# Decoder layer on one core: four chunks of a feed-forward product moved across an all-engine barrier

## The chip, the cores and the metric

One Trainium2 chip, one of its cores. The metric is the device time of one execution in microseconds (us). TensorE (PE) does matmuls and transposes, ScalarE (ACT), VectorE (DVE) and GpSimd (POOL) the elementwise work, SyncE (SP) issues most DMAs. "PEld" rows are weight loads of TensorE.

## The reference, cut to what matters

Input x is 2 batches of 512 rows of 1024. The layer is:

```python
x = layernorm(x + attention(x))
x = layernorm(x + matmul(fake_quant(x), fake_quant(ctx)))        # called x2 below
h = relu(x @ up_w) ** 2                                          # 1024 -> 2048
routed = (x @ fc1_w) @ expert_w * sum(top2(x @ gate_w)) @ fc2_w  # 1024 -> 512 -> 512 -> 1024
x = layernorm(x + layernorm(h @ down_w + routed, gamma, beta))
```

All of it is float32. The change lies in the first tiles of `x @ up_w`, for batch 0.

## The kernel before, in words

The program has two parts, each a block in which every engine runs a list of its own, and engines wait for one another through semaphores. The first part is attention and cross product (to x2), the second the feed-forward layer. At the end of the first block all engines drain and meet (the profile puts this at line 71), and a second meeting follows that clears semaphores (line 2157). Together they are called the barrier here.

Each factor of a product is split into a rounded part (`_hi`) and the rest (`_lo`), and a product is three matmuls, hi x hi, hi x lo and lo x hi, for every chunk k of 128 of the 1024 contracted columns. A 128 x 512 tile of the hidden layer thus takes 8 chunks x 3 = 24 matmuls into one PSUM bank. Weight tiles are numbered m; tile m sits in slot m % 2 of `u_hi` and `u_lo`. Batches are b.

The first block computes x2 for all 8 row tiles. While its last tiles are still in work, TensorE fills in: it transposes batch 0's rows (`x2T_hi`, `x2T_lo`), computes the routing logits of batch 0 (`first_logits`, 16 matmuls) and the products (m, b) = (0, 0) and (1, 0), each in two halves of four chunks (`first_product(m, part)`). The last of a product's matmuls raises `op_used`.

The second block begins with `first_products`: TensorE transposes batch 1's rows chunk by chunk (`transpose_x1(k)`, four transposes each, into three PSUM banks in turn), ScalarE rounds the chunk (`x1T_hi_out`, line 1645), VectorE subtracts (`x1T_lo_out`, line 1809, raises `x1T_lo_done`), and TensorE contracts it for (0, 1) and (1, 1). A contraction (line 1552) of chunk k waits for `x1T_lo_done` k + 1; a transpose of chunk k >= 3 waits for k - 2, since its bank must have been read. After that the products of tiles 2, 3, ... follow, for both batches, then seven block products (line 1611) in phases p1 to p7.

ScalarE's list at the start of the second block, in the order of the code:

```python
x1T_hi_out(0); x1T_hi_out(1); logits_out(0); x1T_hi_out(2); relu(0, 0)
x1T_hi_out(3); square(0, 0); x1T_hi_out(4); relu(1, 0); x1T_hi_out(5)
square(1, 0); x1T_hi_out(6); x1T_hi_out(7)
```

`relu(m, b)` waits for the `op_used` of its product. `split_u(m)` (ScalarE, then VectorE at line 1813) prepares weight tile m once the slot's former products are over. SyncE loads weight tiles 2 and 3 first thing behind the barrier, and SyncE and GpSimd wait there until the stores of x2 have landed.

Of the kernel before, what the change touches and what calls it, by code (L numbers as in the profile page):

```python
# [33 lines left out]
KT = EMB // P  # L34
# [16 lines left out]
def split_products(stationary, moving):  # L51

    (s_hi, s_lo), (m_hi, m_lo) = stationary, moving
    return ((s_hi, m_hi), (s_hi, m_lo), (s_lo, m_hi))


def attention_and_cross(nc, so, args, x2_dram, w2_dram):
# [13 lines left out]
    with ExitStack() as ctx:  # L71
# [82 lines left out]
        S = {**so["sem"], **{n: sem(n) for n in names}}  # L154
# [162 lines left out]
        def _(pe):  # L317
# [76 lines left out]
            def cross(t):  # L394
                pe.wait_ge(S["q1T_done"], t + 1)
                b = t // BT
                for k in range(CK):
                    for n in range(NH):
                        mm = pe.matmul(xa_ps[:, n * BANK:(n + 1) * BANK], q1T[:, t % 2, k], q2[:, b, k, n * BANK:(n + 1) * BANK],
                                       start=(k == 0), stop=(k == CK - 1))  # L400
                mm.then_inc(S["xa_ready"], 1)
# [34 lines left out]
            def first_logits():  # L436
                pe.wait_ge(S["x2T_lo_done"], KT)
                pe.wait_ge(S["gate_lo_done"], 1)
                gate = so["gate_st"]
                rows = lambda n: tr_ps[0:n, 0:BT].rearrange("p t c -> p (t c)")  # L440
                for k in range(KT):
                    pe.matmul(rows(2 * EXPERTS), gate[:, k], x2T_hi[:, k], start=(k == 0), stop=False)
                    mm = pe.matmul(rows(EXPERTS), gate[:, k, 0:EXPERTS], x2T_lo[:, k], start=False, stop=(k == KT - 1))
                mm.then_inc(S["lgT_ready"], 1)

            def first_product(m, part):
                if part == 0:
                    pe.wait_ge(S["u_lo_done"], m + 1)
                    pe.wait_ge(S["o_done"], TILES)
                acc = sc_ps[:, m * NG * TQ // 2:(m + 1) * NG * TQ // 2].rearrange("p n d -> p (n d)")  # L450
                for k in range(part * KT // 2, (part + 1) * KT // 2):
                    pe.wait_ge(S["x2T_lo_done"], k + 1)
                    st = [so[u][:, m, k] for u in ("u_hi", "u_lo")]
                    for i, (s, v) in enumerate(split_products(st, (x2T_hi[:, k], x2T_lo[:, k]))):
                        mm = pe.matmul(acc, s, v, start=(k == 0 and i == 0), stop=(k == KT - 1 and i == 2))
                if part == 1:
                    mm.then_inc(S["op_used"], 1)
# [81 lines left out]
            transpose_x2(7)  # L539
            cross(7)  # L540
            first_product(0, 1)
            first_product(1, 0)
            first_logits()
            first_product(1, 1)

        @block.scalar
        def _(act):
# [721 lines left out]
def product_index(m, b):  # L1269

    return 2 * b + m if m < 2 else 2 * m + b
# [11 lines left out]
def feed_forward(nc, so, args, x2_dram, w2_dram, t_dram, r_dram, x2b_dram, out):  # L1283
# [8 lines left out]
    with ExitStack() as ctx:  # L1292
# [64 lines left out]
        S = {**so["sem"], **{n: sem("f_" + n) for n in names}}  # L1357
# [155 lines left out]
        def _(pe):  # L1513
            def transpose_x1(k):

                if k >= 3:
                    pe.wait_ge(S["x1T_lo_done"], k - 2)
                for t in range(BT):
                    mm = pe.transpose(x1T_bank(k)[:, t * P:(t + 1) * P], x2_tok[:, t, k * P:(k + 1) * P], ident[:])  # L1519
                mm.then_inc(S["x1T_ready"], 1)  # L1520
# [27 lines left out]
            def contraction(m, b, k):  # L1548

                st = [u[:, m % 2, k] for u in (u_hi, u_lo)]  # L1550
                for i, (s, v) in enumerate(split_products(st, (xT_hi[b][:, k], xT_lo[b][:, k]))):
                    mm = pe.matmul(acc_b[:, product_index(m, b) % 4], s, v, start=(k == 0 and i == 0), stop=(k == KT - 1 and i == 2))  # L1552
                return mm

            def first_products():

                for k in range(3):
                    transpose_x1(k)
                pe.wait_ge(S["u_lo_done"], 2)
                for k in range(KT):  # L1560
                    pe.wait_ge(S["x1T_lo_done"], k + 1)
                    mm = contraction(0, 1, k)
                    if k < 3:
                        contraction(1, 1, k)
                    if k + 3 < KT:
                        transpose_x1(k + 3)
                mm.then_inc(S["op_used"], 1)
                for k in range(3, KT):
                    mm = contraction(1, 1, k)
                mm.then_inc(S["op_used"], 1)  # L1570
# [13 lines left out]
            def tile_step(phase, k, t):  # L1584
# [29 lines left out]
                elif t == BT - 1 and k % 2:  # L1614
                    mm.then_inc(S["d_used"], 1)

            first_products()
            transpose_logits(0)
            for m in range(2, MU):
# [565 lines left out]
```

## Time and profile before

| | |
|---|---|
| median of 3 runs | 629.79 us (627.51, 629.79, 632.41) |
| profiled execution | 629.14 us |
| its span, first to last instruction | 627.3 us |
| TensorE busy | 593.6 us, 95% |
| mean granted TensorE clock | 0.992 |
| barrier, TensorE's last matmul to its first transpose | 206.46 to 207.73 us |

Times in the rows are us from the span's start, durations us unless marked ns. An idle time stands in brackets with what ended it. Ends of matmuls are modelled, their starts are recorded. The span is the part of an execution that the rows cover.

### The profile page before, as it was taken

The page shows a single profiled execution, that of the slowest core. Times are in us where ns is not written, and L with a number is a line of the kernel's source. Part 1 is how long each engine was busy: PE and PEld are TensorE (multiplying, and loading weights), DVE is VectorE, ACT ScalarE, POOL GpSimd, SP SyncE. Part 2 cuts the span into 40 slices and gives each one's busy share as a digit, 9 for nine tenths or more (in the row PEclk, how much of TensorE's full clock was granted, in tenths as well). Part 3 has the DMA queues.
Part 4 walks back from the last instruction along what each step waited for, and adds up shares of the span by engine and source line. Part 5 has one row for each costly group of instructions (what it writes and reads, how often), then busy time and mean ns, then how long its engine had stood idle before and what let it go on. Part 6 is the DMA issues. An engine that isn't in the chain of part 4 may idle for free.

```text
span 627.3 us, 9388 instructions
## 1 busy us (share of the span) xinstructions
PE 593.6 (95%) x3728; PEld 476.8 (76%) x3728; DVE 382.1 (61%) x515; ACT 299.1 (48%) x384; POOL 123.9 (20%) x162
## 2 busy tenths in 40 slices
PE   2799999998999899999999999999999999999993
PEld 1687877666776688788888888888888888888882
DVE  4947898889854355335333331338864565749976
ACT  4556688896684544333333342114344333323824
POOL 2811355735442022422210000000000000021000
PEclk9999999998999999999999999999999999999998
DMA  9766675673663668779998774203433336089913
GB/s 335 286 186 187 183 203 167 170 259 106 194 203 135 241 239 317 263 274 344 315 344 314 252 253 121 77 1 101 135 91 86 94 99 235 1 275 328 293 55 124
DMA packets 82252, 123.61 MB, mean 197 GB/s; under 512 B 23840, under 2 KB 50720, under 8 KB 82208
## 3 DMA queue, kind: packets, MB, share of 16 engines
q1 hardware_dynamic: 74592, 94.95, 45.6%
q0 software_dynamic: 5168, 19.40, 9.3%
q10 hardware_dynamic: 2448, 8.65, 4.3%
q8 instruction: 30, 0.49, 0.3%
q14 instruction: 14, 0.11, 0.1%
HBM read 83.13 MB, written 35.65 MB: 189 GB/s over the span
## 4 chain that ended last, share of the span: by engine, by line
PE 65%; DVE 1%; ACT 0%; issue 0%; ACTq 0%
PE psum L1552 33%; PE psum L1611 30%; PE psum L1519 0%; PE psum L1528 0%; PE psum L1527 0%; PE psum L1545 0%; DVE ffn_lo L1959 0%; DVE ffn_lo L1948 0%; ACT hx L1714 0%; ACT ffn_lo L1724 0%; DVE stat_n L1940 0%; DVE ffn_lo L1933 0%; DVE x1T_lo L1809 0%; PE psum L1536 0%; ACT x1T_hi L1645 0%
## 5 line engine op out<-in xcount | busy, mean ns | idle before, releaser
L1813 DVE TENSOR_TENSOR u_lo<-u_raw,u_hi 128x1024 fp32r<-128x1024 f32 x18 | 24.7, 1373 | 73.7 <-ACT u_hi L1650 73.7
L1552 PE MATMUL psum<-x1T_hi,u_hi 128*128 128x512 f32 x160 | 62.9, 393 | 0.7 <-DVE x1T_lo L1809 0.7
L1552 PE MATMUL psum<-x1T_hi,u_lo 128*128 128x512 f32 x160 | 62.3, 389 | 0.0
L1552 PE MATMUL psum<-x1T_lo,u_hi 128*128 128x512 f32 x160 | 62.3, 389 | 0.0
L1611 PE MATMUL psum<-x2T_lo,x2T_hi 128*128 128x512 f32 x264 | 62.1, 389 | 0.0
L1611 PEld LDWEIGHTS psum<-x2T_lo,x2T_hi 128*128 128x128 f32 x264 | 49.6, 188 | 10.3
L1552 PE MATMUL psum<-x2T_hi,u_hi 128*128 128x512 f32 x144 | 56.5, 392 | 0.0
L1552 PE MATMUL psum<-x2T_lo,u_hi 128*128 128x512 f32 x144 | 56.1, 389 | 0.0
L1552 PE MATMUL psum<-x2T_hi,u_lo 128*128 128x512 f32 x144 | 56.0, 389 | 0.0
L2090 POOL DMA_DIRECT2D x1T_hi<-r_scratch x4 | 2.9, 713 | 243.9 <-PE psum L1611 243.9
L1611 PE MATMUL psum<-x1T_hi,x2T_hi 128*128 128x512 f32 x216 | 50.4, 389 | 0.0
L1611 PE MATMUL psum<-x1T_hi,x2T_lo 128*128 128x512 f32 x216 | 50.4, 389 | 0.0
L341 PE MATMUL psum<-w_hi,xT_hi 128*128 128x512 f32 (+1 forms) x128 | 35.5, 359 | 13.0 <-POOL w_lo L1132 8.2
L1611 PEld LDWEIGHTS psum<-x1T_hi,x2T_lo 128*128 128x128 f32 x216 | 40.5, 188 | 8.4
L1611 PEld LDWEIGHTS psum<-x1T_hi,x2T_hi 128*128 128x128 f32 x216 | 40.5, 188 | 8.4
L1552 PEld LDWEIGHTS psum<-x1T_hi,u_hi 128*128 128x128 f32 x160 | 30.1, 188 | 7.4 <-issue 0.9
L1552 PEld LDWEIGHTS psum<-x1T_hi,u_lo 128*128 128x128 f32 x160 | 30.0, 188 | 6.3
L1552 PEld LDWEIGHTS psum<-x1T_lo,u_hi 128*128 128x128 f32 x160 | 30.0, 188 | 5.9
L341 PEld LDWEIGHTS psum<-w_hi,xT_hi 128*128 128x128 f32 x128 | 20.4, 195 | 18.4 <-issue 8.8
L341 PE MATMUL psum<-w_hi,xT_lo 128*128 128x512 f32 (+1 forms) x128 | 34.3, 349 | 0.0
L341 PE MATMUL psum<-w_lo,xT_hi 128*128 128x512 f32 (+1 forms) x128 | 33.8, 346 | 0.0
L1690 ACT ACTIVATE x2T_hi<-f1b 128x1024 fp32r<-128x1024 f32 x12 | 12.7, 1057 | 39.7 <-PE psum L1611 24.5
(258 smaller groups left out, 1237.3 us busy)
## 6 DMA issues: line engine op xcount, KB each, us to landing
d_raw<-in_L_ffn_down_w_dram SPq DMA_DIRECT2D x20, 512.0 KB, 7.7
t_scratch<-d_raw SPq DMA_DIRECT2D x20, 512.0 KB, 5.1
d_raw<-t_scratch SPq DMA_DIRECT2D x20, 512.0 KB, 3.8
c_sb<-in_ctx_dram ACTq DMA_DIRECT2D x16, 512.0 KB, 3.9
u_raw<-in_L_ffn_up_w_dram SPq DMA_DIRECT2D x16, 512.0 KB, 5.2
r_scratch<-f1b SPq DMA_DIRECT2D x10, 512.0 KB, 4.4
r_scratch<-f2b SPq DMA_DIRECT2D x10, 512.0 KB, 3.1
x_sb<-in_x_dram SPq DMA_DIRECT2D x8, 512.0 KB, 5.8
```

Of the source, the lines that this page charges most:

```text
L341: mm = pe.matmul(qkv_ps[:, c0:c1], s, v, start=(k == 0 and i == 0), stop=(k == KT - 1 and i == 2))
L1552: mm = pe.matmul(acc_b[:, product_index(m, b) % 4], s, v, start=(k == 0 and i == 0), stop=(k == KT - 1 and i == 2))
L1611: mm = pe.matmul(acc_of(phase)[:, t], a, v, start=(k == 0 and i == 0), stop=(k == NP - 1 and i == 2))
L1690: act.activation(oa[oa_slot(s)][:, :, 0], a_raw(phase, j), ACT.Copy).then_inc(S["oa_hi_done"], 1)
L1813: dve.tensor_tensor(u_lo[:, m % 2], u_raw[:, m % 2], u_hi[:, m % 2].bitcast(F32), ALU.subtract).then_inc(S["u_lo_done"], 1)
L2090: pool.dma_start(ob[ob_slot(s)].rearrange("p s h c -> p s (h c)"), r_dram[k * P:(k + 2) * P, n].rearrange("(s p) h c -> p s (h c)", p=P)). ...
```

## The change

`first_product(1, 1)`, chunks 4 to 7 of product (1, 0), leaves the first block, and `first_logits` stands ahead of `first_product(1, 0)`. In the second block the same four chunks are contracted behind the transposes of chunks 0 to 2 of batch 1, and chunk 3 is transposed ahead of the last of them; so the transposes in the loop run four chunks ahead of the contraction and not three.

```diff
@@ -539,9 +539,8 @@
             transpose_x2(7)
             cross(7)
             first_product(0, 1)
+            first_logits()
             first_product(1, 0)
-            first_logits()
-            first_product(1, 1)
@@ -1557,13 +1556,18 @@
                 for k in range(3):
                     transpose_x1(k)
                 pe.wait_ge(S["u_lo_done"], 2)
+                for k in range(KT // 2, KT):
+                    mm = contraction(1, 0, k)
+                    if k == KT - 2:
+                        transpose_x1(3)
+                mm.then_inc(S["op_used"], 1)
                 for k in range(KT):
                     pe.wait_ge(S["x1T_lo_done"], k + 1)
                     mm = contraction(0, 1, k)
                     if k < 3:
                         contraction(1, 1, k)
-                    if k + 3 < KT:
-                        transpose_x1(k + 3)
+                    if k + 4 < KT:
+                        transpose_x1(k + 4)
                 mm.then_inc(S["op_used"], 1)
                 for k in range(3, KT):
                     mm = contraction(1, 1, k)
```

## Rows read from the trace of the kernel before

**Rows 1.** The page: the chain that ended last, shares of the span by line.

```profile
PE psum L1552 33%; PE psum L1611 30%; PE psum L1519 0%; PE psum L1528 0%; PE psum L1527 0%; PE psum L1545 0%; DVE ffn_lo L1959 0%; DVE ffn_lo L1948 0%; ACT hx L1714 0%; ACT ffn_lo L1724 0%; DVE stat_n L1940 0%; DVE ffn_lo L1933 0%; DVE x1T_lo L1809 0%; PE psum L1536 0%; ACT x1T_hi L1645 0%
```

**Rows 2.** Stretches of the span: busy time of each engine, TensorE clock, DMA share, GB/s.

```profile
206.47:207.73 1.26, 0.00 (x1) 0.04 (x1) 0.00 (x0) 0.00 (x0) 0.00 (x0) 1.00 0.00 0
207.73:209.94 2.21, 1.50 (x12) 1.28 (x13) 1.06 (x4) 1.46 (x4) 0.80 (x1) 1.00 0.27 78
209.94:223.98 14.04, 14.01 (x73) 11.12 (x73) 5.83 (x8) 9.35 (x17) 0.81 (x2) 1.00 0.89 325
223.98:616.70 392.72, 392.67 (x1742) 323.23 (x1740) 216.45 (x280) 144.04 (x188) 35.36 (x33) 1.00 0.57 194
```

**Rows 3.** TensorE in order of time: start us, us, line, operation, count, idle before it.

```profile
203.58 0.39 PE L455 MATMUL psum<-x2T_hi,u_hi 128*128 128x512 f32 x1
...
206.07 0.39 PE L455 MATMUL psum<-x2T_hi,u_lo 128*128 128x512 f32 x1
207.73 1.50 PE L1519 MATMUL psum<-ident,f2b 128*128 128x128 f32 x12 [1.26 <-PEq L2157]
209.94 0.47 PE L1552 MATMUL psum<-x1T_hi,u_hi 128*128 128x512 f32 x1 [0.72 <-DVE x1T_lo L1809]
210.25 0.40 PE L1552 MATMUL psum<-x1T_lo,u_hi 128*128 128x512 f32 x1
...
211.18 0.40 PE L1552 MATMUL psum<-x1T_hi,u_lo 128*128 128x512 f32 x1
211.41 0.60 PE L1519 MATMUL psum<-ident,f2b 128*128 128x128 f32 x4
211.77 0.47 PE L1552 MATMUL psum<-x1T_hi,u_hi 128*128 128x512 f32 x1
...
217.33 0.60 PE L1519 MATMUL psum<-ident,f2b 128*128 128x128 f32 x4
...
218.92 0.40 PE L1552 MATMUL psum<-x1T_hi,u_lo 128*128 128x512 f32 x1
219.34 0.50 PE L1552 MATMUL psum<-x1T_hi,u_hi 128*128 128x512 f32 x1
219.68 0.40 PE L1552 MATMUL psum<-x1T_lo,u_hi 128*128 128x512 f32 x1
```

**Rows 4.** Drains at line 71: duration min/median/max in ns, then the start in us.

```profile
L71 ACTq DRAIN  x1: 1271/1271/1271, 197.5 to 197.5; - x1
L71 POOLq DRAIN  x1: 667/667/667, 199.0 to 199.0; - x1
L71 DVEq DRAIN  x1: 853/853/853, 199.7 to 199.7; - x1
L71 SPq DRAIN  x1: 124/124/124, 200.9 to 200.9; - x1
L71 PEldq DRAIN  x1: 4295/4295/4295, 202.2 to 202.2; - x1
```

**Rows 5.** Two stretches around the end of the last store of x2.

```profile
202.00:203.00 1.00, 1.00 (x6) 0.43 (x5) 0.00 (x0) 0.00 (x0) 0.00 (x0) 1.00 0.57 234
203.00:204.00 1.00, 1.00 (x6) 0.65 (x4) 0.00 (x0) 0.00 (x0) 0.00 (x0) 1.00 0.00 0
```

**Rows 6.** VectorE in order of time, ahead of the barrier and behind it.

```profile
192.52 1.22 DVE L931 TENSOR_TENSOR u_lo<-u_raw,u_hi 128x1024 fp32r<-128x1024 f32 x1
...
209.11 2.11 DVE L1809 TENSOR_TENSOR x1T_lo<-psum,x1T_hi 128x512 fp32r<-128x512 f32 x3 [1.05 <-ACT x1T_hi L1645]
...
218.59 0.69 DVE L1809 TENSOR_TENSOR x1T_lo<-psum,x1T_hi 128x512 fp32r<-128x512 f32 x1 [0.43 <-ACT x1T_hi L1645]
221.92 1.23 DVE L1813 TENSOR_TENSOR u_lo<-u_raw,u_hi 128x1024 fp32r<-128x1024 f32 x1 [2.63 <-ACT u_hi L1650]
```

**Rows 7.** TensorE in order of time around 145 us.

```profile
145.43 0.62 PE L381 MATMUL psum<-ident_bf,q 128*128 128x128 bf16 x8 [1.79 <-ACT q L578]
```

**Rows 8.** The stretch behind that: TensorE's busy time, then its granted clock.

```profile
146.00:150.00 4.00, 3.62 (x66) 0.57 0.38 139
```

## Prediction

> **What bounds the kernel now.** I read the chain that ended last first. It is TensorE nearly throughout: the first products (line 1552) and the matmuls of the seven block products (line 1611) make 63% of the span [rows 1]. The windows say how full TensorE is there: from 223.98 to 616.70 it is busy 392.67 of 392.72 us, at a granted clock of 1.00 [rows 2]. So time saved ahead of 223.98 reaches the end whole, and nothing behind that point has slack that could swallow it. The windows ahead of it show what is still to be had: 1.26 us in which TensorE stands at the barrier, then 2.21 us of which 1.50 is busy, then 14.04 us that look full [rows 2]. I then read TensorE in order of time. The barrier's gap lies between the last matmul of `first_product(1, 1)`, which starts at 206.07, and the first transpose at 207.73; twelve transposes follow, and the first contraction starts at 209.94, released by VectorE's `x1T_lo` [rows 3]. A second stall hides in the window that looks full: the matmul before it starts at 218.92, the next at 219.34, where the step is 0.23 [rows 3]. Last, the drains at line 71 say who opens the barrier: ScalarE's ends at 198.8, GpSimd's at 199.7, VectorE's at 200.6, SyncE's at 201.0, TensorE's at 202.2 + 4.3 = 206.5 [rows 4]. TensorE alone holds the barrier for the last 5.5 us.
>
> **Removed ahead of the barrier.** `first_product(1, 1)` is four chunks of three matmuls, 12 in all. From 203.58 to 206.07 are 11 steps, 0.226 each [rows 3]; 12 x 0.226 = 2.72 us. The 16 logit matmuls are moved ahead of `first_product(1, 0)`, on the same engine and at the same cost, with nothing that they read late: VectorE had finished the last of its work for them and for the second weight slot at 192.52 + 1.22 = 193.74 [rows 6], and they would start near 203.58 - 16 x 0.23 - 2.72 = 197.2. With 12 matmuls fewer TensorE arrives at 203.8 and is still 2.8 us behind SyncE, so the barrier opens 2.72 us earlier.
>
> **Added behind it.** The same 12 matmuls, between the transposes of chunks 0 to 2 and the first contraction of batch 1. Their moving rows and weights are ready since before the barrier, so they wait for nothing. There the step is a little longer: 210.25 to 211.18 is four steps, 0.2325 each [rows 3]. 12 x 0.2325 = 2.79 us, 0.07 more than was removed. Each group of four transposes costs 0.36 us to the next matmul (211.41 to 211.77) and 0.08 more at that matmul (209.94 to 210.25 is 0.31 against 0.23) [rows 3]. There are six such groups in both kernels (chunks 0 to 2 together, then 3, 4, 5, 6 and 7), so they cancel.
>
> **The first stall goes.** TensorE waits for chunk 0's transpose, ScalarE's rounding and VectorE's subtraction. How long, a row bounds from two sides. By the modelled end of the transposes it is the 0.72 of the row. By starts it is more: a group of four has 0.60 busy, but its successor starts after 0.36, 0.24 before that end; so the twelve, 1.50 busy, would let a matmul start at 207.73 + 1.50 - 0.24 = 208.99, and the stall is 209.94 - 208.99 = 0.95 us [rows 3]. I take 0.95, since starts are observed and a successor was seen to start ahead of the modelled end. [...]
>
> **The second stall goes too, if the copies keep pace.** Chunk 7's transposes start at 217.33 and its contraction at 219.34, 2.01 us later, with 9 matmuls between them (218.59 + 0.69 = 219.28 is the end of VectorE's last `x1T_lo`) [rows 3, 6]. The stall is 219.34 - 218.92 - 0.23 = 0.19, and 0.11 more at the matmul behind it (219.68 - 219.34 against 0.23): 0.30 us. After the change the transposes run one chunk further ahead. Counted from the first transpose behind the barrier: transposes of 0 to 2 until 1.26 (0.95 earlier than 2.21); 9 moved matmuls 0.08 + 2.09, to 3.43; chunk 3's transposes to 3.79; 3 moved matmuls to 4.57; six matmuls for k = 0 to 5.97, then chunk 4's transposes; 1.84 each for k = 1 and 2 with their transposes, so chunk 5 at 7.81 and chunk 6 at 9.65; three matmuls, and chunk 7's transposes at 10.79 to 11.15; nine matmuls for k = 4, 5, 6, to 13.32. Chunk 7 is ready at 10.79 + 2.01 = 12.80: 0.52 us of slack where there was none. The other waits in that stretch have more: chunk 3's transposes need `x1T_lo` of chunk 0, ready at 2.21 (before: 209.94), at 3.43; k = 6 starts at 12.62 and needs 9.65 + 2.01 = 11.66.
>
> **Waits and queues that move.** One wait becomes real: ScalarE's `relu(1, 0)` waits for the second `op_used`, which was up before the barrier and now comes at about 4.8 on the scale above. ScalarE reaches it behind its copy of chunk 4, whose transposes start at 5.97, so near 7.2: no wait, and the square and the copies of 5 to 7 queued behind it are not held. TensorE's product of the third weight tile needs `u_lo`, written at 221.92 + 1.23 = 223.15 against a start of 223.98, 0.83 to spare [rows 2, 6]; it hangs on the end of contraction (0, 1), behind which the same 15 matmuls and 4 logit transposes follow as before, so the 0.83 stays. Every load that SyncE or GpSimd issues behind the barrier starts 2.72 us earlier while its reader moves by less, so none gets later. They wait for the stores of x2; DMA is busy 0.57 of the stretch from 202 to 203 and nothing from 203 to 204 [rows 5], and the barrier would open at 207.73 - 2.72 = 205.0. I cost all of this at nothing; if that cover were gone, up to the 0.52 and 0.83 would be eaten before anything shows.
>
> **The sum.** 0.95 + 0.30 - 0.07 = 1.18 us. The profiled execution took 629.14 (span 627.3 and 1.8 around it); it would take 627.96. The median of the three runs is 629.79, 0.65 above the profiled one, so I forecast 628.6. Bounds of the gain: 0.65 (0.72 - 0.07, the second stall unchanged) to 1.25 (no loss in the step), so 628.5 to 629.1.
>
> **Rivals.**
> [...]
> Another engine opens the barrier. Then the 12 matmuls are added and not moved: 2.72 - 1.18 = 1.54 us slower, 631.3. That is the price if some drain ends at 206.5; from 205.0 (203.8 + 1.18) on the change loses. The latest is at 201.0 [rows 4], so this is unlikely.
> The copies fall behind: ScalarE does the same list in a shorter time after the transposes come. If chunk 7 is 0.5 us late beyond its slack, about the size of the stall now, the gain is near 0.7: 629.1.
> Nothing is gained, since a wait that I did not see (`u_lo` of the third tile, a weight load) ends last again at 223.98: 629.8. For it speaks only that the stall's place would move; against it the 0.83 and the earlier loads.
>
> **How the numbers follow.** Forecast 0.60 (628.6); copies behind 0.12 (629.1); clock, faster 0.11 (626.9); clock, slower 0.07 (630.3); nothing gained 0.06 (629.8); barrier held 0.04 (631.3). The three runs shown lie from 627.51 to 632.41, so a median can sit a us or two from its place. The range takes in all cases but the last with that scatter: 626.3 to 631.3. About 1% (6.3 us) is what a measurement of this kernel can tell from no change; no case above reaches it, so within 1% gets 0.95, and faster and slower keep 0.02 and 0.03 for what I did not see.
>
> **What would show it.** Right: line 71's TensorE drain ends near 203.8 and is still last; the first transpose starts near 205.0; the first matmul behind the twelve transposes is of the moved product and starts within 1.3 us of it; the first contraction of batch 1 shows no wait for `x1T_lo`, and neither does k = 7; the third tile's product starts near 222.8. Wrong: a drain of another engine later than TensorE's, a clock under 1.00 between 203 and 215, or a start of the third tile's product at 223.9 or later. A difference of several us in the time, with these rows as forecast, would be scatter between runs and not this change.

## The result, and the profile after

| | before | changed |
|---|---|---|
| median | 630.57 us (14 runs, 627.51 to 635.05) | 627.71 us (14 runs, 625.77 to 630.69) |
| profiled execution, its span | 629.14, 627.3 us | 630.69, 628.9 us |

The ratio of changed to before is 0.9964, with an interval from 0.9946 to 0.9981: 1.2 to 3.4 us faster at 630.57. Two further measurements of the same kernel gave 0.9984 (0.9962 to 1.0006) and 0.9974 (0.9954 to 0.9993), so 1.0 and 1.6 us; the first of these two intervals includes 1, which is no change. The gain is small, and the forecast was 1.18. That it is real rests on the stretch D below more than on the medians.

The profiled execution of the changed kernel is, at 628.9, longer than that of the kernel before at 627.3. Whoever compares spans alone sees a loss. The chain that ended last is TensorE as before, with the lines shifted (1552 is now 1551, 1611 is 1615). Shares of the span by line:

```profile
PE psum L1551 33%; PE psum L1615 30%; PE psum L1518 1%; PE psum L1526 0%; PE psum L1527 0%; PE psum L1544 0%; DVE ffn_lo L1963 0%; DVE ffn_lo L1952 0%; ACT hx L1718 0%; ACT ffn_lo L1728 0%; DVE stat_n L1944 0%; DVE ffn_lo L1937 0%; PE psum L1535 0%; ACT root_f L1721 0%; DVE rstd_f L1970 0%
```

Against [rows 1], `DVE x1T_lo` and `ACT x1T_hi`, the copies that TensorE waited for, are gone from the list, and the chain no longer passes through them. The windows that answer to [rows 2], cut at the same events (same columns):

```profile
206.66:207.89 1.23, 0.00 (x0) 0.03 (x1) 0.00 (x0) 0.00 (x0) 0.00 (x0) 1.00 0.00 0
207.89:209.15 1.26, 1.26 (x12) 1.26 (x13) 0.22 (x2) 0.50 (x2) 0.52 (x1) 1.00 0.12 21
209.15:225.63 16.48, 16.48 (x87) 13.45 (x85) 6.67 (x9) 10.29 (x19) 2.47 (x3) 1.00 0.80 286
225.63:618.30 392.67, 392.66 (x1742) 323.23 (x1740) 214.46 (x279) 143.96 (x188) 34.50 (x33) 1.00 0.57 194
```

The barrier's gap is as before (1.23 against 1.26), the transposes behind it are followed at once, and the long window is busy for all of its 16.48 us. Behind 225.63 TensorE is as full as it was, 392.66 of 392.67 us. TensorE in order of time, as in [rows 3]:

```profile
206.27 0.39 PE L455 MATMUL psum<-x2T_hi,u_lo 128*128 128x512 f32 x1
207.89 1.50 PE L1518 MATMUL psum<-ident,f2b 128*128 128x128 f32 x12 [1.24 <-PEq L2161]
209.15 0.47 PE L1551 MATMUL psum<-x2T_hi,u_hi 128*128 128x512 f32 x1
209.47 0.39 PE L1551 MATMUL psum<-x2T_lo,u_hi 128*128 128x512 f32 x1
...
211.31 0.60 PE L1518 MATMUL psum<-ident,f2b 128*128 128x128 f32 x4
211.67 0.48 PE L1551 MATMUL psum<-x2T_hi,u_hi 128*128 128x512 f32 x1
...
212.45 0.40 PE L1551 MATMUL psum<-x1T_hi,u_hi 128*128 128x512 f32 x1
...
218.61 0.60 PE L1518 MATMUL psum<-ident,f2b 128*128 128x128 f32 x4
...
220.89 0.39 PE L1551 MATMUL psum<-x1T_hi,u_lo 128*128 128x512 f32 x1
221.11 0.39 PE L1551 MATMUL psum<-x1T_hi,u_hi 128*128 128x512 f32 x1
...
225.63 0.50 PE L1551 MATMUL psum<-x2T_hi,u_hi 128*128 128x512 f32 x1
```

A moved matmul starts 1.26 us behind the first transpose (207.89 to 209.15) where TensorE stood until 2.21 before. The first contraction of batch 1 (212.45) and the last chunk's (221.11, 0.22 behind the matmul ahead of it) carry no wait. From the first transpose to the third weight tile's product are 225.63 - 207.89 = 17.74 us; before it was 16.25, without the 12 matmuls. The drains at line 71, as in [rows 4]:

```profile
L71 ACTq DRAIN  x1: 1271/1271/1271, 200.4 to 200.4; - x1
...
L71 PEldq DRAIN  x1: 4270/4270/4270, 202.4 to 202.4; - x1
L71 DVEq DRAIN  x1: 853/853/853, 202.6 to 202.6; - x1
L71 SPq DRAIN  x1: 123/123/123, 203.8 to 203.8; - x1
```

TensorE's ends at 206.7, still the last, but now only 2.8 us behind SyncE's at 203.9; it was 5.5. All of them are 3 us later than I had written, since this execution lost time far ahead of the change. At least part of that is TensorE's clock, which fell to 0.50 twice in its first 40 us (in each row: TensorE's busy time, then the mean granted clock, the DMA's share, GB/s):

```profile
22.00:24.00 2.00, 1.54 (x5) 0.59 1.03 395
24.00:26.00 2.00, 2.00 (x12) 0.55 0.45 114
32.00:34.00 2.00, 1.38 (x4) 0.65 0.34 56
34.00:36.00 2.00, 2.00 (x9) 0.50 0.32 50
```

An estimate from these rows is that up to 3.4 us of work are lost (2 x 0.41 + 2 x 0.45 + 2 x 0.35 + 2 x 0.50), where by the same count the execution before lost 1.7, at 146 to 150 [rows 8]. The other 1.2 us or so of the 2.9 us delay are not explained.

So I measure the change by one stretch that holds all of its edits: **D**, from the first matmul of product (0, 0)'s second half, which both kernels run right behind the last cross product, to the first of the third weight tile. Before: 194.22 to 223.98, 29.76 us. After: 197.13 to 225.63, 28.50 us. What lies behind D is 403.3 us in both (627.3 - 223.98, 628.9 - 225.63), and 403.2 to 403.3 in every run below; D is 1.26 shorter. Counted from D's start the forecast's moments are met: TensorE's drain ends at 9.54 (forecast 203.8 - 194.22 = 9.6), the first transpose starts at 10.76 (10.8), the third tile's product at 28.50 (28.6).

### The profile page after: what moved, and what is told of

It reads as the page before. It is cut to its first block, busy times and chain, and to the rows that moved or that the text cites. A ratio compares the mean times of both kernels' runs of the same rounds, so it can differ in the third digit from the quotient of the medians.

```text
span 628.9 us, 9377 instructions
## 1 busy us (share of the span) xinstructions
PE 593.1 (94%) x3718; PEld 477.5 (76%) x3728; DVE 378.4 (60%) x515; ACT 298.7 (47%) x384; POOL 121.9 (19%) x162
## 4 chain that ended last, share of the span: by engine, by line
PE 65%; DVE 1%; ACT 0%; issue 0%
PE psum L1551 33%; PE psum L1615 30%; PE psum L1518 1%; PE psum L1526 0%; PE psum L1527 0%; PE psum L1544 0%; DVE ffn_lo L1963 0%; DVE ffn_lo L1952 0%; ACT hx L1718 0%; ACT ffn_lo L1728 0%; DVE stat_n L1944 0%; DVE ffn_lo L1937 0%; PE psum L1535 0%; ACT root_f L1721 0%; DVE rstd_f L1970 0%
## 5 line engine op out<-in xcount | busy, mean ns | idle before, releaser
L1551 PE MATMUL psum<-x2T_hi,u_hi 128*128 128x512 f32 x148 | 58.2, 393 | 0.0
L1551 PE MATMUL psum<-x2T_hi,u_lo 128*128 128x512 f32 x148 | 57.6, 389 | 0.0
L1551 PE MATMUL psum<-x2T_lo,u_hi 128*128 128x512 f32 x148 | 57.6, 389 | 0.0
L1551 PEld LDWEIGHTS psum<-x2T_hi,u_lo 128*128 128x128 f32 x148 | 27.8, 188 | 5.9
```

## The experiments

**Both kernels again.** No edit.

> The kernel before, unchanged, as a second profile of it and as a measure of scatter. The measure of all these runs is D, the time from the first matmul of product (0, 0)'s second half (line 455, start 194.22 in the kernel before) to the first matmul of the third weight tile (start 223.98): 29.76 us before, 28.50 after (197.13 to 225.63), so 1.26 us gained. Theory A (the gain is the two stalls of TensorE behind the barrier and nothing else): D is 29.8 within 0.1, clock 1.00 between first and last of it, and the ratio of times is 1.000. Theory B (executions of the kernel before often lose time to a clock fall at the barrier, which makes up the difference between the 1.3 us of the profiles and the 2.3 us of the ratio): a granted clock under 1.00 between 205 and 215 and D near 31.5.

> The changed kernel, unchanged, as a second profile of it. Theory A: D is 28.5, no fall of the clock in it, and the median lies 1.2 us under the kernel before. Theory B: D is 28.5 too, but the median lies 2 to 2.5 us under it.

> The changed kernel once more, beside the held one on the same chip, for its scatter and a third profile. Theory A (two stalls, 1.2 us): the ratio to the kernel before is 0.998, within the scatter of its first two measurements, 0.9964 and 0.9984. Theory C: in one profile or another VectorE's u_lo takes 2.4 us and D is 28.9 or more.

Measured: the kernel before against itself gives the ratio 1.0011 (0.9988 to 1.0035) and D 29.76, with its start at 194.24. The changed one has D 28.52 with its start at 193.59, and D 28.53 with its start at 196.32. The clock was 1.00 through D in all five profiles of the two kernels. So theory B has nothing for it: no profile of the kernel before shows a fall at the barrier. D repeats to 0.03 us, and what scatters between executions is its start, the part of the program ahead of every edit. Clock falls are likely one source of that: the changed kernel's second profile shows none ahead of D (1.00 in every stretch up to 193.5) and starts D first, at 193.59; the third shows one, between 30 and 36 us (0.71, 0.50 and 0.94 in its three stretches of 2 us), and starts it at 196.32. A gain of 1.26 of 630 is a ratio of 0.9980, and this lies in all three intervals. The executions whose mean granted clock is on record (87 of the kernel before, 38 of the changed) allow one more comparison, an estimate: a straight line through time against mean clock, with one step for the change, puts the changed kernel 1.3 us lower at equal clock, with a standard error of 0.2. It is rougher than D: the same line gives 0.6 us slower (error 0.4) for the run below that only transposes further ahead, whose D is 0.34 shorter. Theory C's long `u_lo` (VectorE's work on the third weight tile held up by GpSimd, found in the run that moves the matmuls alone) did not appear in these three profiles, but see below how close it was.

**The logits alone**, against the kernel before:

```diff
-            first_product(1, 0)
             first_logits()
+            first_product(1, 0)
             first_product(1, 1)
```

> The kernel before with one edit: the 16 logit matmuls stand ahead of product (1, 0), all of which stays ahead of the barrier. Theory A: nothing, D is 29.76 within 0.1. Rival (the logits' place matters, since ScalarE copies them out behind the barrier): D differs by 0.3 or more.

Measured, in one profiled execution: D 29.75. The logits' place is worth nothing.

**The move alone**, with the transposes three chunks ahead as before (the edit is shown against the changed kernel):

```diff
                 for k in range(KT // 2, KT):
                     mm = contraction(1, 0, k)
-                    if k == KT - 2:
-                        transpose_x1(3)
...
-                    if k + 4 < KT:
-                        transpose_x1(k + 4)
+                    if k + 3 < KT:
+                        transpose_x1(k + 3)
```

> The twelve matmuls are moved, but the transposes run three chunks ahead as before, not four. Theory A: the first stall (0.95 us) goes, the second (0.30 us at the last chunk) stays, 0.07 is lost to the longer step: D is 29.76 - 0.88 = 28.9, and chunk 7's contraction waits for VectorE. Rival (the copies are held by something else, and moving the matmuls frees ScalarE too): D is 28.5 as with the whole change. In the time: 0.9 us under before, too little to tell from 1.2.

Measured: D 29.30, a gain of 0.46 and not 0.88; the ratio 1.0009 (0.9986 to 1.0031) can't tell either from nothing. The first stall is gone and the second is there, as expected (matmul, last chunk's matmul, then the logit transposes and the third tile's product; TensorE in order of time):

```profile
219.93 0.40 PE L1551 MATMUL psum<-x1T_hi,u_lo 128*128 128x512 f32 x1
220.35 0.50 PE L1551 MATMUL psum<-x1T_hi,u_hi 128*128 128x512 f32 x1
...
224.68 0.42 PE L1535 MATMUL psum<-ident,hx 16*128 16x16 f32 x4
225.47 0.47 PE L1551 MATMUL psum<-x2T_hi,u_hi 128*128 128x512 f32 x1 [0.38 <-ACT f2b L1657]
```

219.93 to 220.35 is the second stall, 0.42 for 0.23; VectorE's copy of that chunk ends at 220.30. New is the last row: 0.79 from the logit transposes to the product, where it is 0.35 in the kernel before. The trace names ScalarE's write of `f2b`, which ended last by its records, but the product doesn't wait for that in the code; it waits for `u_lo_done`. VectorE's row in that execution, and GpSimd's:

```profile
222.93 2.39 DVE L1815 TENSOR_TENSOR u_lo<-u_raw,u_hi 128x1024 fp32r<-128x1024 f32 x1 [2.63 <-ACT u_hi L1652]
```

```profile
221.84 2.41 POOL L2076 TENSOR_TENSOR s_own<-s_own,hx 128x1024 f32<-128x1024 f32 x1 [5.72 <-DMA s_own<-x_scratch]
```

VectorE's subtraction took 2.39 us, from 222.93 to 225.32; in D of every other kernel it takes 1.23. GpSimd's addition of beta to the first tile of x2 had started at 221.84 and ran until 224.25; VectorE ended 1.07 behind that, and the product started 0.15 behind VectorE. The same two engines in the changed kernel (the first row is the last chunk's copy):

```profile
219.88 0.69 DVE L1813 TENSOR_TENSOR x1T_lo<-psum,x1T_hi 128x512 fp32r<-128x512 f32 x1 [0.44 <-ACT x1T_hi L1649]
223.57 1.23 DVE L1817 TENSOR_TENSOR u_lo<-u_raw,u_hi 128x1024 fp32r<-128x1024 f32 x1 [3.00 <-ACT u_hi L1654]
```

```profile
223.99 3.05 POOL L2078 TENSOR_TENSOR s_own<-s_own,hx 128x1024 f32<-128x1024 f32 x1 [6.97 <-DMA s_own<-x_scratch]
```

Here VectorE began first, by 0.42 us, kept its 1.23, and GpSimd took 3.05 instead of 2.4. In the kernel before, VectorE was first by 1.8 (221.92 against 223.72). In both executions the engine that began first kept its time, and the later one took its own time and the overlap, less 0.16: VectorE in the run of the move alone 1.23 + 1.32 - 0.16 = 2.39, GpSimd in the changed kernel 2.4 + 0.81 - 0.16 = 3.05. Behind D it happens too: in the second profile of the changed kernel a `u_lo` of 2.99 us begins at 234.94 beside an addition that began at 234.46, and costs nothing, since what lies behind D took 403.3 us there as everywhere. The trace of the kernel before had it already, in rows that the prediction did not look at:

```profile
236.79 3.42 DVE L1813 TENSOR_TENSOR u_lo<-u_raw,u_hi 128x1024 fp32r<-128x1024 f32 x1 [4.61 <-ACT u_hi L1650]
```

```profile
236.74 2.39 POOL L2074 TENSOR_TENSOR s_own<-s_own,hx 128x1024 f32<-128x1024 f32 x1 [6.55 <-DMA s_own<-x_scratch]
```

VectorE began 0.05 us behind GpSimd there and took 3.42 us (1.23 + 2.34 - 0.16 = 3.41), and GpSimd kept its 2.39.

**The move alone, and the changed kernel, with GpSimd held** until `u_lo` is written:

```diff
                 pool.wait_ge(xb_in, 16 * (n + 1))
+                if n == 0:
+                    pool.wait_ge(S["u_lo_done"], 3)
```

> The run with the matmuls moved and the transposes three ahead, with the same hold on GpSimd. Theory C: u_lo takes 1.23 us, the product of the third tile waits for nothing, and D falls from 29.30 to 28.85; what is left over the 28.50 of the changed kernel is the second stall, 0.30. Rival (the copies or the reordered transposes made that wait): D stays at 29.3.

> The changed kernel, with GpSimd's first addition held until VectorE has written u_lo of the third weight tile. Theory C (VectorE and GpSimd shut each other out: in the run that only moved the matmuls, VectorE's u_lo began while GpSimd's addition ran, took 2.39 us in place of 1.23 and held TensorE for 0.45; in the changed kernel GpSimd begins only 0.4 us after VectorE): D is 28.5 as in the profiles of the changed kernel, u_lo takes 1.23, GpSimd's addition begins behind its end and takes 2.4 and not 3.05. In the time: under the changed kernel by up to 0.3 if some of its executions pay the 0.45, else the same. Rival (the 2.39 had another cause): u_lo is long in some profile in spite of the hold.

Measured with the move alone: D 28.82, the product waits for nothing, and the rows of VectorE and GpSimd are:

```profile
221.87 1.23 DVE L1815 TENSOR_TENSOR u_lo<-u_raw,u_hi 128x1024 fp32r<-128x1024 f32 x1 [2.63 <-ACT u_hi L1652]
```

```profile
223.25 2.39 POOL L2078 TENSOR_TENSOR s_own<-s_own,hx 128x1024 f32<-128x1024 f32 x1 [8.11 <-DVE u_lo L1815]
```

VectorE is back at 1.23, GpSimd at 2.39. The hold did that and not chance: GpSimd's load was issued at 214.59 and landed 6.2 us later, at 220.8, so without the hold the addition would have begun about 1 us ahead of `u_lo`, as it did in the run without it. Theory C holds: 29.30 - 28.82 = 0.48 us was the clash. The changed kernel with the hold: D 28.54, `u_lo` 1.23 and the addition 2.39 us, ratio 0.9980 (0.9958 to 1.0001), beside 0.9974 for the same kernel without it. The hold gains nothing that can be measured, which fits that the three profiles of the changed kernel all fell on the good side, VectorE ahead by 0.42, 0.50 and 0.15 us. That some of its executions fall on the other is likely with such margins, but no profile shows one.

**Four chunks ahead, nothing moved**, against the kernel before:

```diff
+                    if k == 0:
+                        transpose_x1(3)
                     mm = contraction(0, 1, k)
...
-                    if k + 3 < KT:
-                        transpose_x1(k + 3)
+                    if k + 4 < KT:
+                        transpose_x1(k + 4)
```

> Nothing is moved across the barrier; only the transposes run four chunks ahead (chunk 3 ahead of the first contraction of batch 1). Theory A: the first stall stays at about 0.95, the second goes: D is 29.76 - 0.30 = 29.5. Rival (the two stalls are one chain, and with the first still there the copies stay late): D is 29.7 or more. The time is 0.3 us under before or the same, inside the scatter.

Measured: D 29.42, a gain of 0.34, with the first stall still at 0.72 in its row (now ahead of chunk 3's transposes) and no wait at the last chunk. The time can't tell (1.0008, 0.9985 to 1.0031). The stalls are two and not one chain.

**One chunk moved in place of four**, chunk 3 transposed right behind it. Against the changed kernel; in the first block `first_product(1, 1)` stands again and leaves out its last chunk (not shown):

```diff
-                for k in range(KT // 2, KT):
-                    mm = contraction(1, 0, k)
-                    if k == KT - 2:
-                        transpose_x1(3)
+                mm = contraction(1, 0, KT - 1)
                 mm.then_inc(S["op_used"], 1)
+                transpose_x1(3)
```

> Only the last chunk of product (1, 0), 3 matmuls (0.70 us), is moved, and chunk 3 is transposed behind it; the transposes run four chunks ahead. Theory A (the first stall is 0.95 us measured by starts): chunk 3's transposes wait for chunk 0 until 2.21 after the first transpose, then take 0.36, so the first contraction of batch 1 starts at 2.6 in place of 2.21 with 0.70 of moved work ahead of it; the gain is 0.3 to 0.6: D is 29.2 to 29.5. If the stall were the 0.72 of the modelled end, the three moved matmuls would fill it and chunk 3's transposes would show no wait.

Measured, in one profiled execution: D 28.62, nearly all of the gain, against an expected 29.2 to 29.5. TensorE in order of time:

```profile
210.60 1.50 PE L1521 MATMUL psum<-ident,f2b 128*128 128x128 f32 x12 [1.24 <-PEq L2162]
211.86 0.47 PE L1554 MATMUL psum<-x2T_hi,u_hi 128*128 128x512 f32 x1
...
212.39 0.40 PE L1554 MATMUL psum<-x2T_hi,u_lo 128*128 128x512 f32 x1
212.73 0.66 PE L1521 MATMUL psum<-ident,f2b 128*128 128x128 f32 x4
213.14 0.47 PE L1554 MATMUL psum<-x1T_hi,u_hi 128*128 128x512 f32 x1
```

The expectation was mis-added. It charged chunk 3's transposes to the stall, but they are work that stands elsewhere in the kernel before, so they fill it as the moved matmuls do. The three matmuls take 0.76 (0.31 + 0.22 + 0.23) of the 0.95, and what is left of the stall is 0.11 ahead of chunk 3's transposes, which wait for the copy of chunk 0 (0.34 from the last matmul, for 0.23), and 0.05 behind them (0.41 for 0.36). That they waited at all speaks for 0.95: a stall of 0.72 would have been filled by 0.76.

**Eight and twelve chunks moved.** Eight: all of product (1, 0). Twelve: the second half of product (0, 0) as well, contracted ahead of it, with its own `op_used`. First the edit for eight against the changed kernel, then what twelve adds:

```diff
             first_logits()
-            first_product(1, 0)
...
-                for k in range(KT // 2, KT):
+                for k in range(KT):
                     mm = contraction(1, 0, k)
```

```diff
-            first_product(0, 1)
             first_logits()
...
+                for k in range(KT // 2, KT):
+                    mm = contraction(0, 0, k)
+                mm.then_inc(S["op_used"], 1)
                 for k in range(KT):
                     mm = contraction(1, 0, k)
```

> All 8 chunks of product (1, 0), 24 matmuls, stand behind the barrier, among the transposes. TensorE then arrives 5.4 us earlier than in the kernel before, which is where SyncE's drain ends (201.0 against 206.5). Theory A with TensorE as the one who opens the barrier: TensorE and SyncE arrive within 0.3 us of each other, D is 28.5 + 0.07 (the longer step) + at most 0.3 = 28.5 to 28.9, no further gain, since the stalls are gone already. Rival (the barrier costs more when all engines arrive at once, or another engine is last already): D is 29.5 or more.

> Also the second half of product (0, 0) stands behind the barrier: 36 matmuls moved in all, 8.2 us. Theory A with the point from which the barrier's rival decides: SyncE's drain is now last, by 8.2 - 5.4 = 2.7 us, TensorE stands idle for that time ahead of the barrier, and D is 28.5 + 0.1 + 2.7 = 31.3 (counted from the first logit matmul plus the 12 matmuls that stood ahead of it), that is 1.5 us slower than before. With 4 us of idle in a row the granted clock may fall, which would add up to 1.7. Rival (the barrier is not held by SyncE, the first block's tail ends earlier): D stays near 28.6.

Measured with eight: D 28.56, ratio 0.9963 (0.9944 to 0.9982). The drains of TensorE and SyncE:

```profile
L71 PEldq DRAIN  x1: 4333/4333/4333, 198.2 to 198.2; - x1
...
L71 SPq DRAIN  x1: 123/123/123, 202.3 to 202.3; - x1
```

TensorE's ends at 202.5 and SyncE's at 202.4: a tie, at no cost that can be told (the barrier's gap is 1.66 us between starts, against 1.62). GpSimd's addition is over here before `u_lo` begins (219.11 + 2.39 = 221.50 against 222.19), so the two don't meet. With twelve: ratio 1.006 (1.004 to 1.008), 3.8 us slower than before, and D 33.91, which was expected at 31.3. The drains, TensorE in order of time, and its clock:

```profile
L71 PEldq DRAIN  x1: 4315/4315/4315, 193.7 to 193.7; - x1
...
L71 SPq DRAIN  x1: 123/123/123, 200.6 to 200.6; - x1
```

```profile
197.62 0.39 PE L443 MATMUL psum<-x2T_lo,gate_st 128*8 128x512 f32 x1
201.93 2.36 PE L1516 MATMUL psum<-ident,f2b 128*128 128x128 f32 x10 [3.92 <-PEq L2162]
```

```profile
200.00:201.00 1.00, 0.00 (x0) 0.97 0.00 0
201.00:202.00 1.00, 0.07 (x1) 0.50 0.95 393
...
206.00:207.00 1.00, 1.00 (x3) 0.50 1.23 313
207.00:208.00 1.00, 1.00 (x4) 0.61 0.97 338
208.00:209.00 1.00, 1.00 (x6) 1.00 0.95 365
```

SyncE now opens the barrier, 2.7 us behind TensorE, and the gap grows from 1.62 to 4.31 us between starts. That gives 28.50 + 2.69 = 31.2, the expected part. The other 2.7 are the clock: it falls to 0.50 at 201, after TensorE has stood for 3 us (its last matmul ends at 198.01), and comes back in the window from 207 to 208, at about 207.8. TensorE is busy from 201.93 on, 5.8 us of it at 0.50, where its matmuls start 0.43 apart (204.94, 205.37, 205.80) and not 0.23, as from 208.09 on. The estimate from that is about 2.9 us of work lost, and 2.7 show in D. I had expected at most 1.7, the price of the one fall in [rows 8].

## Why the prediction was right

The measured median, 627.71, is 0.9 under the 628.6 of the forecast and in the range; the ratio's interval begins at 1.2 us, where the forecast's 1.18 stands. How near the median came is partly luck: the forecast started from 629.79, a median of three runs, where 14 runs gave 630.57, and the changed kernel's first median was lower than its next two (628.91 and 628.71). What bears the prediction out is D, which takes the first block's scatter out. Its terms are:

- **Removed ahead of the barrier, 2.72 us, and TensorE opens it.** TensorE's drain is the last in every kernel with up to four moved chunks, and the tie with eight and the loss with twelve put the limit where the drains of [rows 4] had it, 5.4 us of removed work. The barrier's gap itself shrank by 0.04 between starts (1.66 to 1.62), a term that the sum doesn't have.
- **Added behind it, 2.79.** The rows of the moved matmuls give 2.16 + 0.78 - 2 x 0.08 = 2.78 (209.15 to 211.31 and 211.67 to 212.45, less the 0.08 behind each group of transposes), against 2.72 removed: 0.06 for the forecast's 0.07. The runs can't resolve it: D repeats to 0.03, and of the 0.06 that eight chunks cost against four, 0.04 is the barrier's gap.
- **The first stall, 0.95.** The moved matmul starts 1.26 behind the first transpose, as worked out; 2.21 - 1.26 = 0.95. The choice of starts over the modelled end was right.
- **The second stall, 0.30.** The four-ahead transposes alone gave 0.34. The table of starts (chunk 3's transposes at 3.43, the next at 5.97, 7.81, 9.65, 10.79) met the trace's 3.42, 5.94, 7.76, 9.58, 10.72. The last chunk's contraction had 221.11 - (218.61 + 2.01) = 0.49 to spare, for 0.52. ScalarE's `relu(1, 0)` began 7.07 behind the first transpose, forecast near 7.2, and waited for nothing; `u_lo` of the third tile was written at 224.80, 0.83 ahead of its product, as forecast.
- **The sum.** 1.18 forecast, 1.23 to 1.26 in D over three profiles. The three ratios average 0.9974, or 1.6 us, 0.4 more than D explains, which is less than the intervals' width. I can't say that it is scatter alone, only that nothing in the stretches behind the edits shows it, and that at equal mean clock the estimate is 1.3.
- **One step was argued badly, at no cost here: the loads were costed at nothing.** It said: "Every load that SyncE or GpSimd issues behind the barrier starts 2.72 us earlier while its reader moves by less, so none gets later." None did. But an earlier load makes its reader run earlier, and GpSimd's addition came closer to VectorE's `u_lo`, from 1.8 us behind it (2.1 in the second profile) to 0.15 to 0.5. Both hang on the barrier: the addition starts about 16 us behind the first transpose in both kernels (15.99 and 16.25, then 15.86 to 16.20), while `u_lo` moved from 14.19 to 15.7 behind it, since the moved matmuls now stand between. The spare 0.83 us at `u_lo` is not enough for a clash: the product starts 0.15 behind the write, so 0.68 is free, and the clash adds 1.16 to the subtraction, 0.48 to D. In D of the changed kernel's three profiles GpSimd paid for the overlap and VectorE didn't, so the 0.83 was enough only because VectorE still began first. Why the load landed earlier in the run that moved the matmuls alone (its addition began 14.9 behind the first transpose) stays open.
- **The clock.** The two clock cases of the forecast, 626.9 and 630.3, take 1.72 us for a fall. That is an estimate from 4 us at 0.57 on the mean (4 x 0.43) [rows 8], behind an idle time of 1.79 us [rows 7]; no run shows a fall of that price at the barrier. The clock held 1.00 there in all 12 profiles with a gap of 1.6 to 1.7 us between starts. With 4.31, in the run that moves twelve chunks, it fell to 0.50 and cost 2.7 us. This change set off no fall there in its three profiles, and 1.72 was 1 us too low for the one that was seen.

## What to carry to other kernels

Where one engine opens a barrier alone, work can be taken from ahead of it and put behind it at almost no price (0.06 us for 12 matmuls here), and the gain is the idle time that it fills there, not the work moved: 3, 12 and 24 moved matmuls all gave 1.1 to 1.3 us. Read the other engines' drains first, since they say how much can be taken; past that point (5.4 us here) each microsecond moved becomes idle time, and with a gap of 4.31 us between starts the clock fell to 0.50 as well. Little filler does it: three matmuls and a group of transposes gave 1.14 of 1.26 us, with the transposes one chunk further ahead in that run too. When a moved block makes transfers earlier, look for what their readers then run into, and when two medians differ by less than the scatter, find the stretch that holds all of the edits and measure that.

## What the runs showed of the hardware

VectorE's subtraction `u_lo` (128 x 1024, fp32) took 2.39 us in place of 1.23 when it began while GpSimd's addition ran, and GpSimd's took 2.98 to 3.33 in place of 2.4 when it began 0.15 to 0.5 us behind VectorE's: in each of these pairs the later one paid, the length of the overlap less about 0.15 us, and the first kept its 1.23 or 2.4. In the kernel before the same pair cost VectorE 3.42 us at 236.79. After an idle of 4.3 us between starts TensorE's clock stood at 0.50 from 201.0 to 207.8, although it was busy again from 201.9. That fall cost 2.7 us of D, where the one in [rows 8] is worth 1.7.
